# A graph layer on one core: mix product and output projection of the last edge pass as three passes over rounded parts

## What is computed

```python
qkv = x @ W_qkv.T + b_qkv
att = jnp.einsum('mhd,mhd->mh', Q[receivers], K[senders]) * INV_SQRT_DK
...
out = jax.ops.segment_sum(attention[:, :, None] * V[senders], receivers, num_segments=N)
return out.reshape(N, H * DV) @ W_ff.T + b_ff
...
W = (edge_feats @ W_dist + b_dist) * cut[:, None]
msgs = x_j * W
agg = jax.ops.segment_sum(msgs, receivers, num_segments=node_feats.shape[0])
out = jnp.concatenate([node_feats, agg], axis=1) @ W_comb + b_comb
...
x = _layernorm(x + _L0_gnn_ref(x, edge_index, ...), axis=-1)
x = _layernorm(x + _L1_gnn_ref(node_type_100, x, src, dst, ...), axis=-1)
```

## Time and profile before

| | |
|---|---|
| time, median of 3 runs | 1166.85 us (1166.7 to 1167.99) |
| the profiled execution: its own time, its span | 1165.22 us, 1163.5 us |
| PE busy | 1072.6 us (92% of the span) |
| DVE busy | 987.6 us (85%) |
| ACT busy | 799.1 us (69%) |
| POOL busy | 694.1 us (60%) |
| last edge pass, 990 to 1020 us: PE, DVE, ACT, POOL busy | 30.0, 26.0, 17.2, 13.8 of 30 us |

### The profile page before, as it was taken

One profiled execution on the slowest core, in us unless ns is written; L12 is line 12 of the kernel. 1 busy time (PEld: TensorE's weight loads), 2 busy tenths in 40 slices (PEclk: granted clock), 3 DMA queues, 4 the chain that ended last, 5 costly groups with the idle time before them and its releaser, 6 DMA issues.

```text
span 1163.5 us, 24929 instructions
## 1 busy us (share of the span) xinstructions
PE 1072.6 (92%) x7106; PEld 987.7 (85%) x7106; DVE 987.6 (85%) x2646; ACT 799.1 (69%) x2464; POOL 694.1 (60%) x558
## 2 busy tenths in 40 slices
PE   4959999999999999999887878879999999999994
PEld 3759999999999999999666767668888888888883
DVE  4978888888888888887989899868888888888882
ACT  2857777777777777777778878884555555555553
POOL 4367777777777777775777776413444444444442
PEclk9979999999999999999989999989999999999997
DMA  4856666666666666665545556646666666666740
GB/s 147 274 210 211 229 226 225 229 232 221 220 219 218 218 228 229 224 224 179 199 148 179 181 183 224 235 154 168 174 171 177 182 183 185 187 185 180 185 139 33
DMA packets 121385, 227.23 MB, mean 195 GB/s; under 512 B 33587, under 2 KB 61486, under 8 KB 121184
## 3 DMA queue, kind: packets, MB, share of 16 engines
q1 hardware_dynamic: 104000, 189.54, 49.0%
q0 software_dynamic: 17248, 36.08, 11.4%
HBM read 137.84 MB, written 93.59 MB: 199 GB/s over the span
## 4 chain that ended last, share of the span: by engine, by line
PE 78%; DVE 8%; issue 6%; ACT 3%; DMA 2%; POOL 1%; SPq 1%; DVEq 0%; POOLq 0%; ACTq 0%
PE ps L938 14%; PE ps L920 7%; PE ps L818 5%; PE ps L797 5%; PE ps L812 4%; PE ps L811 4%; PE ps L856 4%; PE ps L855 4%; PE ps L857 4%; PE ps L813 4%; PE ps L969 4%; PE ps L853 2%; DVE stat L1340 2%; DVE yn L1368 2%; PE ps L962 2%
## 5 line engine op out<-in xcount | busy, mean ns | idle before, releaser
L696 POOL TENSOR_TENSOR zin<-xin,bff_row 128x1024 f32<-128x1024 f32 x98 | 233.4, 2384 | 78.6 <-DVE stat L1340 62.7
L818 PE MATMUL ps<-w_mix,zT 128*128 128x256 f32 x780 | 193.5, 396 | 33.8 <-ACT zT L1046 32.7
L818 PEld LDWEIGHTS ps<-w_mix,zT 128*128 128x128 f32 x780 | 146.2, 196 | 62.9 <-ACT zT L1046 41.8
L1368 DVE SCALAR_TENSOR_TENSOR yn<-ps,r,bc 128x256 f32<-128x256 f32 x391 | 169.2, 473 | 28.6 <-PE ps L813 15.3
L1062 ACT ACTIVATE junk<-yn 128x256 f32<-128x256 f32 x391 | 158.1, 416 | 45.6 <-DVE yn L1368 45.3
L715 POOL TENSOR_TENSOR ev<-abc,v 128x512 f32<-128x512 f32 x49 | 66.2, 1353 | 198.1 <-DVE zeT L1560 198.1
L1340 DVE BATCH_NORM_STATS2 stat<-zin 128x6 f32<-128x256 f32 x391 | 136.2, 409 | 9.4 <-POOL zin L696 9.4
L705 POOL DMA_INDIRECT xd<-in_x_dram,idx x98 | 94.2, 961 | 78.3 <-PE ps L841 47.0
L1075 ACT ACTIVATE on<-yn,r 128x256 f32<-128x256 f32 x293 | 126.7, 501 | 0.0
L721 POOL DMA_INDIRECT out_dram<-oe,idx x98 | 98.1, 1001 | 33.8 <-issue 22.1
L811 PE MATMUL ps<-mix_hi,z_hi 128*128 128x256 f32 x392 | 114.8, 293 | 2.6 <-DVE z_lo L1405 2.6
(11 more groups left out here) (202 smaller groups left out, 3079.4 us busy)
## 6 DMA issues: line engine op xcount, KB each, us to landing
xin<-in_x_dram SPq DMA_DIRECT2D x97, 512.0 KB, 4.7
out_dram<-on SPq DMA_DIRECT2D x97, 512.0 KB, 2.9
xd_o<-xdT SPq DMA_DIRECT2D x49, 256.0 KB
v_o<-vT SPq DMA_DIRECT2D x49, 256.0 KB, 2.0
v<-v_o SPq DMA_DIRECT2D x49, 256.0 KB
abc<-a_o SPq DMA_DIRECT2D x196, 64.0 KB
xd<-xd_o SPq DMA_DIRECT2D x49, 256.0 KB, 4.3
sbc<-same_o SPq DMA_DIRECT2D x49, 128.0 KB, 4.0
```

The lines of the kernel that those rows point to most:

```text
L696: pool.tensor_tensor(z, xx, bb, ALU.add).then_inc(n_z, 1)
L818: last = mm(ps[0:np_, half(g, j), (j % 2) * D:(j % 2 + 1) * D], zT[:, g % 2, k, j * P:j * P + np_], w_mix[:, k, :], start=k == 0, stop=k = ...
L1368: last = dve.scalar_tensor_tensor(out=yn[0:np_, q, j * D:(j + 1) * D], in0=ps[0:np_, half(g, j), (j % 2) * D:(j % 2 + 1) * D], scalar=r1[0 ...
```

## The change

The output projection `ff` and the mix product `mix` no longer take float32 operands. Each of their four products becomes three float32r products: high part by high part, high by low, low by high. For that the running sums `num` and the rows `zeT` are split in every step: ACT writes the rounded high part (`sum_high(i)`, `edge_z_high(i-1)`, a copy of 128x512), and POOL subtracts it from the full value for the low part (`sum_low(i)`, `edge_z_low(i-1)`). The parts have one buffer each; they lie in `z_lo`, a tile of the node pass that is free by then, and appear under that name in the trace. The projection's weights are split once, in the node pass (one more DVE subtraction of 128x256 for each half).

```diff
+    ze_hi, ze_lo = (z_lo[:, 0, c, :].rearrange("p (c n) -> p c n", c=2) for c in range(DC))
+    num_hi, num_lo = (z_lo[:, 1, c, :].rearrange("p (c n) -> p c n", c=2) for c in range(DC))
...
+        def edge_z_low(n):
+            pool.wait_ge(e_z, 2 * (n + 1))
+            pool.wait_ge(e_zh, n + 1)
+            after(pool, e_mixp, n)
+            pool.tensor_tensor(flat(ze_lo), flat(zeT[:, n % 2]), flat(ze_hi), ALU.subtract).then_inc(e_zl, 1)
+
+        def sum_low(n):
+            pool.wait_ge(e_num, 2 * (n + 1))
+            pool.wait_ge(e_nh, n + 1)
+            after(pool, e_ffp, n)
+            pool.tensor_tensor(flat(num_lo), flat(num[:, n % 2]), flat(num_hi), ALU.subtract).then_inc(e_nl, 1)
...
             if within(i + 1):
                 weigh(i + 1)
+            if within(i):
+                sum_low(i)
+            if within(i - 1):
+                edge_z_low(i - 1)
...
         def ff(n):
             par = n % 2
-            pe.wait_ge(e_num, 2 * (n + 1))
+            pe.wait_ge(e_nh, n + 1)
+            pe.wait_ge(e_nl, n + 1)
             after(pe, e_z, 2 * (n - 1))
             for c in range(2):
+                to = bank(FF[par])[:, c, :]
                 for k in range(DC):
-                    last = mm(bank(FF[par])[:, c, :], wff[:, k, c * P:(c + 1) * P], num[:, par, k, :], start=k == 0, stop=k == DC - 1)
+                    hi, lo = (w[:, k, c * P:(c + 1) * P] for w in (wff_hi, wff_lo))
+                    mm(to, hi, num_hi[:, k, :], start=k == 0, stop=False)
+                    mm(to, hi, num_lo[:, k, :], start=False, stop=False)
+                    last = mm(to, lo, num_hi[:, k, :], start=False, stop=k == DC - 1)
             last.then_inc(e_ffp, 1)
...
         def mix(n):
             after(pe, e_y, 2 * n)
-            rows_product(bank(MIX), zeT[:, n % 2], w_mix, False).then_inc(e_mixp, 1)
+            pe.wait_ge(e_zh, n + 1)
+            pe.wait_ge(e_zl, n + 1)
+            for t in range(2):
+                for k in range(DC):
+                    hi, lo = (a[:, k, t * P:(t + 1) * P] for a in (ze_hi, ze_lo))
+                    mm(bank(MIX)[:, t, :], hi, mix_hi[:, k, :], start=k == 0, stop=False)
+                    mm(bank(MIX)[:, t, :], hi, mix_lo[:, k, :], start=False, stop=False)
+                    last = mm(bank(MIX)[:, t, :], lo, mix_hi[:, k, :], start=False, stop=k == DC - 1)
+            last.then_inc(e_mixp, 1)
...
+        def edge_z_high(n):
+            act.wait_ge(e_z, 2 * (n + 1))
+            after(act, e_mixp, n)
+            act.activation(flat(ze_hi), flat(zeT[:, n % 2]), ACT.Copy).then_inc(e_zh, 1)
+
+        def sum_high(n):
+            act.wait_ge(e_num, 2 * (n + 1))
+            after(act, e_ffp, n)
+            act.activation(flat(num_hi), flat(num[:, n % 2]), ACT.Copy).then_inc(e_nh, 1)
...
             if within(i - 3):
                 edge_final(i - 3)
+            if within(i):
+                sum_high(i)
+            if within(i - 1):
+                edge_z_high(i - 1)
             if within(i - 2):
                 edge_std1(i - 2)
                 agg_term(i - 2)
...
+            dve.tensor_tensor(wff_lo[:, k, :], ps[:, A + 1, D:2 * D], wff_hi[:, k, :], ALU.subtract).then_inc(s_wlo, 1)
...
-            after(dve, e_ffp, n - 1)
+            after(dve, e_nh, n - 1)
+            after(dve, e_nl, n - 1)
...
-            after(dve, e_mixp, n - 1)
+            after(dve, e_zh, n - 1)
+            after(dve, e_zl, n - 1)
```

More of the change, by code:

```diff
@@ L123, in build @@
     z_lo = sb("z_lo", [P, 2, DC, ROWS * P], F32R)
-    wff = sb("wff", [P, DC, D])
+    wff_hi, wff_lo = (sb(n, [P, DC, D], F32R) for n in ("wff_hi", "wff_lo"))
     wd = sb("wd", [RBF + 1, D])
@@ L363, in build @@
     e_zp = sem("edge_z_transposed")
+    e_nh = sem("attention_sum_high_parts")
+    e_nl = sem("attention_sum_low_parts")
+    e_zh = sem("edge_z_high_parts")
+    e_zl = sem("edge_z_low_parts")
     e_st = sem("edge_stats")
@@ L830, in weight_transposes @@
             after(pe, s_wtc, 3 * k)
-            after(pe, s_wlo, 2 * k)
+            after(pe, s_wlo, 3 * k)
             for r in range(4 * DC):
@@ L996, in _ @@
                 pe.wait_ge(s_wtc, 6)
-                pe.wait_ge(s_wlo, 4)
+                pe.wait_ge(s_wlo, 6)
                 pe.wait_ge(s_brow, 2)
@@ L1083, in weight_copies @@
             act.activation(w_hi[:, k, 2 * D:3 * D], ps[:, A + 1, 0:D], ACT.Copy).then_inc(s_wtc, 1)
-            act.activation(wff[:, k, :], ps[:, A + 1, D:2 * D], ACT.Copy).then_inc(s_wtc, 1)
+            act.activation(wff_hi[:, k, :], ps[:, A + 1, D:2 * D], ACT.Copy).then_inc(s_wtc, 1)
         def parts(n):
```

## The result

| | before | changed |
|---|---|---|
| median of 4 runs each | 1167.42 us (1166.7 to 1170.97) | 1204.82 us (1200.56 to 1218.07) |
| the profiled execution: its own time, its span | 1165.22, 1163.5 us | 1200.56, 1198.7 us |
| one steady step of the last edge pass | 7.42 us | 7.96 us |

The changed kernel is slower, by a ratio of 1.0345 (95% interval 1.0304 to 1.0387). The forecast was 1202 us.

What follows compares the result with a forecast made beforehand. PE bound the kernel at 7.42 us a step, DVE's loop close at 7.25. Forecast: 34.5 us for 47 steps at 8.1, plus 0.5 and 0.4, gives 1200.6; the median, 1.6 above, 1202 us, range 1180 to 1215.

Steps and rivals of the forecast that it cites:

- The bound before: Last edge pass: PE full at 7.42 us a step, DVE's loop with ACT at 7.25, so at most 0.17 gained.
- TensorE's gain: Projection and mix: twelve float32r products in 1.41 us replace 1.73 twice a step; PE's work falls 0.64 to 6.78.
- ACT's copies: Two copies between oe and esd, 0.47 us each, 0.94 together, fit 1.08 us of idle time and cost nothing.
- sign (4): In the changed profile, ACT's esd comes no later against zeT than 2.11 us.
- POOL's price and the collision: Each POOL subtraction 1.29 us; edge_z_low, running 3.58 to 4.87 after zeT, holds DVE's scans num; step 8.1 us.
- my allowance of some hundredths for two waits: Two more semaphore waits on POOL add some hundredths to the 8.06 us loop, taken as 8.1.
- sign (3): First scan num recorded at up to 1.5 us instead of 0.73, second normal, no semaphore wait named.
- The sum: 47 steps add 34.5 us, the end 0.5, the node pass weight subtractions 0.4: +35.4 on 1165.22, or 1200.6.
- The end after block 47: edge_z_high(48) puts a copy between the last but one mix product and its ye: 0 to 1.4 us, taken 0.5.
- The first: Rival, chance 0.20: scans not held; a two-step path through four engines takes 15.35 us, 7.68 a step, 1182 us.
- The second: Rival, chance 0.12: first scan num slips in before edge_z_low, second is held; step 8.4, 1214 us or somewhat more.
- TensorE's gain to be had: Rival, chance 0.04: DVE's 7.25 us loop sets the pace, 1162 us; needs POOL subtractions of 0.4 instead of 1.29.

Runs made afterwards that it cites:

- no_sum_low: The changed kernel without POOL's subtraction sum_low, its products running over other data; 1161.83 us against 1163.38 for the kernel before, ratio 0.9971, step 7.25 us.
- mix_only: The changed kernel with only the mix product in three passes, the projection in float32 as before; 1159.06 us against 1167.41 for before, ratio 0.9936.
- spare_fills: The kernel before with two unused POOL fills (memset) added behind each step's weighting; 1166.64 us against 1166.21, ratio 1.0002, step 7.42 us.
- order_alone: The kernel before, float32 products kept, with instructions reordered on POOL, TensorE, ACT and DVE; 1167.22 us against 1167.41, ratio 1.0, step 7.42 us.
- the eleven kernels above: All follow-up variants of the kernel before or the changed kernel, with work added, removed or reordered; measured from 1141.16 to 1219.44 us.
- no_z_low: The changed kernel without POOL's subtraction edge_z_low, its products running over other data; 1219.44 us against 1163.38 for before, ratio 1.048.

## Why the prediction was right

**The bound before.** PE full and DVE's loop just below: right. The loop of 7.25 us appeared whenever nothing else bound (`no_sum_low`, `mix_only`), and 7.42 where TensorE's work was unchanged and nothing was held (`spare_fills`, `order_alone`).

**TensorE's gain.** Twelve products in 1.41 us: in the changed kernel `ff` to the transposes took 1.51 with its first product after a pause, and `mix` 1.42. TensorE's work of 6.8 us a step was confirmed where it bound again (6.79). The chain that ended last shows the idle time, 0.91 us and a first product prolonged to 0.35, where I had 1.3:

```profile
1002.79 0.22 PE ps L989 x2
1003.01 0.91 issue
1003.91 0.35 PE ps L945
```

The first product takes 0.35 instead of 0.12, so about 1.14 us of a step is lost in all. Most of the missing 0.16 is the 0.14 us by which the step came out shorter than forecast.

**ACT's copies.** Expected 0.47 each within 1.08 us of idle time. They take about 0.52, and the second one waited for the mix product, so that `esd` came 2.27 us after `zeT`, 0.16 later than before. That misses the prediction's sign (4), no later than 2.11:

```profile
1002.02 0.63 ACT L1170 ACTIVATE z_lo<-zeT 128x512 fp32r<-128x512 f32 x1 [0.18 <-PE ps L977]
1002.55 0.28 ACT L1165 ACTIVATE esd<-emv,eps_col 128x2 f32<-128x2 f32 x1
```

The lateness is hidden: the scans behind it are held for longer anyway.

**POOL's price and the collision.** 1.29 us for each subtraction was taken; from start to start `ev` takes 1.24 and `sum_low` 1.23, and `edge_z_low` is recorded at 1.29, so it ended 4.79 us after `zeT` and not 4.87. The release 0.18 us before the recorded end measured 0.19. So the loop is 4.79 less 0.19 plus 3.36, or 7.96, for 8.1 forecast; without my allowance of some hundredths for two waits it would have been 8.06, and no run shows that these waits cost anything. The first scan is recorded at 1.31 us, within the "up to 1.5" of sign (3). `edge_z_low` began 0.53 us before the scans and not 0.3, because the subtractions were shorter and the scans 0.15 us later.

**The sum.** It came out at the right place with terms that were off in both directions. `zeT` of blocks 0 and 47 in the changed kernel, for the earlier trace rows:

```profile
793.59 0.88 DVE L1612 SCALAR_TENSOR_TENSOR zeT<-ps,bff_col,xd 128x256 f32<-128x256 f32 x2 [0.53 <-PE ps L947]
...
1167.70 0.86 DVE L1612 SCALAR_TENSOR_TENSOR zeT<-ps,bff_col,xd 128x256 f32<-128x256 f32 x2
```

The 47 steps gave 27.9 us (374.11 less 346.19) for 34.5 forecast. The end after block 47 gave 2.2 (31.0 less 28.8) for 0.5, outside the 0 to 1.4 that I had allowed. The place was right: `ye` of block 47 came 4.80 us after the last `zeT` instead of 3.07, because ACT's copy stands before `esd` and waits for the mix product:

```profile
1176.32 0.63 ACT L1170 ACTIVATE z_lo<-zeT 128x512 fp32r<-128x512 f32 x1 [2.40 <-PE ps L977]
```

And `zeT` of block 0 came 5.1 us later, for 0.4. That last term I cannot attribute: in the eleven kernels above it came anywhere from 784.3 to 793.9 us, with and without the weights' split. In the profiled execution this spread happened to fill what the steps lacked, which is luck: the steps and the end alone make 30.1 us, or 1195.3. Likewise the median lies 4.3 us above the profiled execution and not 1.6. So the path, the wait and the price of a step were right, and that the sum missed the profiled execution by nothing (1200.6 forecast, 1200.56 measured) says less than it seems.

**The rivals.** The first, a path of two steps through four engines, is real but lay below the collision; it shows by its alternating steps once `edge_z_low` is gone. Its price of 7.68 us a step agrees with the estimate from the rows of that run, but left out that TensorE's idle time in it costs the clock and that `hot` is held. The second, one scan slipping in ahead, did not occur in steady steps: `edge_z_low` began 0.53 us before the scan. For TensorE's gain to be had, subtractions of 0.4 us were not needed, as the prediction said of the order it had; another order did it.

## What to carry to other kernels

Where POOL and DVE share the work on SBUF tiles, plan when they run and not how much each has to do: a scan of DVE with two SBUF inputs (`num`, `agg`) or the tensor_scalar `hot` from SBUF to SBUF was held until about 0.19 us before the recorded end of a POOL instruction that reads SBUF, `hot` once by a fill too, and the trace shows it as a longer record without any wait for it. Look for DVE records longer than their siblings, and ask of each added POOL instruction what DVE wants to start while it runs. A gain on the full engine is worth only the distance to the next loop, here 0.17 us a step, until that loop is reordered too.

## What the hardware showed that I had not expected

An idle time of TensorE of 1.7 us before `ff` was followed by a granted clock of 0.54 for 3.2 us in `no_z_low`, while 0.9 us of idle time in every step of the changed kernel left it at 1.00, and so did a single one of 1.9 us near its end; removing work from POOL therefore made the kernel slower (`no_z_low`, 1219 against 1205 us in the changed kernel, each beside its own runs of before: ratios 1.048 and 1.0345). Two POOL instructions in direct succession kept a scan of DVE waiting through both in two profiles (4.03 us for a pair of 1.37), while in the changed kernel a scan once ran between two of them. Fills on POOL, 2.8 us of a step, did not touch the scans, but one of them held `hot` (2.74 us for 0.35).
